# Window graph block and inverted residual on one core: the self part by chunk, w1 rows computed once, and the last depthwise tap as a GpSimd product added by DMA

## What is computed

```python
y = affine(conv1x1(x, fc1_w, fc1_b), fc1_s, fc1_t)
idx = top 9 neighbours of each node by cosine distance   # the node itself is one of them
feat = concat([x_i, x_j - x_i])                          # 9 neighbours j of each node i
h = max over the 9 of gelu((feat @ ew + eb) * es + et)   # 192 channels
x1 = affine(conv1x1(h, fc2_w, fc2_b), fc2_s, fc2_t) + x
```

```python
h = relu(bn(w1 @ x1))
h = relu(bn(depthwise 3x3 convolution of h))             # 9 taps per channel
out = x1 + bn(w2 @ h)
```

## Time and profile before

| what | value |
|---|---|
| median of 3 runs | 4308.5 us (4302.23 to 4312.94) |
| the profiled execution, own time | 4302.27 us |
| its span | 4300.5 us |
| TensorE clock granted, mean | 0.992 |
| PE busy, matmuls | 4078.2 us, 26688 instructions |
| DVE busy | 4077.2 us, 5296 instructions |
| ACT busy | 3620.3 us, 7141 instructions |
| POOL busy | 538.3 us, 548 instructions |
| HBM read and written | 77.68 MB and 25.69 MB |

### The profile page before, as it was taken

The page is one execution under the profiler, slowest core; times in us unless marked ns, Lnnn a source line. Parts: engine busy times, 40 slices in busy tenths (PEclk is TensorE's granted clock), DMA queues, the critical chain, the costliest instruction groups (busy, mean ns, idle before and its releaser), DMA issues.

```text
span 4300.5 us, 84159 instructions
## 1 busy us (share of the span) xinstructions
PE 4078.2 (95%) x26688; PEld 2423.2 (56%) x26688; DVE 4077.2 (95%) x5296; ACT 3620.3 (84%) x7141; POOL 538.3 (13%) x548
## 2 busy tenths in 40 slices
PE   5999999999999999999999999999999999999994
PEld 2555555555555555555555555555555555555552
DVE  2599999999999999999999999999999999999998
ACT  3888888888888888888888888888889888888873
POOL 0011111011111011111011111111111111110100
PEclk9999999999999999999999999999999999999997
DMA  1111121111111111120111111111111111211111
GB/s 48 23 31 33 25 45 18 33 38 30 35 31 31 27 38 32 26 44 16 36 36 24 43 27 32 29 33 34 29 40 20 37 33 25 45 18 25 31 21 24
DMA packets 52989, 134.11 MB, mean 31 GB/s; under 512 B 7778, under 2 KB 9058, under 8 KB 46372
## 3 DMA queue, kind: packets, MB, share of 16 engines
q0 software_dynamic: 28672, 50.35, 8.2%
q1 hardware_dynamic: 23876, 78.22, 6.8%
HBM read 77.68 MB, written 25.69 MB: 24 GB/s over the span
## 4 chain that ended last, share of the span: by engine, by line
PE 61%; ACT 13%; issue 12%; DVE 12%; DMA 0%; SPq 0%; DVEq 0%; ACTq 0%; POOL 0%; POOLq 0%
PE pg L572 15%; DVE acc L954 9%; PE pmisc L498 8%; PE pmisc L482 8%; PE pg L575 7%; PE pvu L559 7%; ACT MV L746 3%; PE pself L586 3%; ACT acc L779 2%; PE pmisc L450 2%; ACT g L763 2%; PE pmisc L500 2%; PE pvu L545 2%; PE pmisc L443 2%; PE pmisc L465 1%
## 5 line engine op out<-in xcount | busy, mean ns | idle before, releaser
L954 DVE SCALAR_TENSOR_TENSOR acc<-hpad,w,acc 128x1024 f32<-128x1024 f32 (+1 forms) x2560 | 2911.9, 1168 | 89.1 <-ACT acc L779 86.0
L572 PE MATMUL pg<-MV,VU 128*128 128x512 f32 x2048 | 1143.8, 640 | 15.6 <-ACT VU L754 14.8
L763 ACT ACTIVATE g<-pg 128x512 f32<-128x512 f32 x1536 | 916.0, 596 | 144.3 <-PE pg L575 75.7
L941 DVE TENSOR_REDUCE hid<-g 128x192 f32<-128x1728 f32 x512 | 992.9, 1939 | 0.0
L746 ACT ACTIVATE MV<-pvu,cst 64x512 f32<-64x512 f32 x1024 | 695.6, 679 | 12.4 <-PE pvu L545 0.2
L482 PE MATMUL pmisc<-x,w 96*128 96x384 f32 (+1 forms) x1536 | 571.6, 487 | 23.1 <-ACT hpad L693 18.5
L575 PE MATMUL pg<-MV,VU 128*64 128x512 f32 x2048 | 527.5, 592 | 0.0
L498 PE MATMUL pmisc<-acc,w 128*96 128x256 f32 x2048 | 494.8, 385 | 30.2 <-ACT acc L786 30.2
L693 ACT ACTIVATE hpad<-pmisc,sh,sc 128x384 f32<-128x384 f32 (+1 forms) x768 | 480.6, 661 | 20.1 <-DVE acc L954 12.7
L559 PE MATMUL pvu<-wVU,y 97*64 97x192 f32 x4096 | 446.6, 339 | 30.6 <-ACT MV L746 30.1
L498 PEld LDWEIGHTS pmisc<-acc,w 128*96 128x96 f32 x2048 | 331.2, 164 | 212.4 <-issue 108.6
(11 more groups left out here) (95 smaller groups left out, 4231.9 us busy)
## 6 DMA issues: line engine op xcount, KB each, us to landing
xin<-in_x_dram SPq DMA_DIRECT2D x32, 768.0 KB, 5.7
invb<-rows_dram SPq DMA_DIRECT2D x32, 768.0 KB
x<-in_x_dram POOLq DMA_DIRECT2D x128, 192.0 KB, 3.6
res<-x POOLq DMA_DIRECT2D x128, 192.0 KB, 3.5
out_dram<-res SPq DMA_DIRECT2D x128, 192.0 KB, 2.1
g<-in_consts_dram SPq DMA_DIRECT2D x1, 640.0 KB
w<-in_p_dram SPq DMA_DIRECT2D x1, 618.5 KB
rows_dram<-norm_rows SPq DMA_DIRECT2D x32, 16.0 KB, 1.4
```

The costliest lines, as they stand in the source:

```text
L572: last = nc.tensor.matmul(ps[:, :], VU[:, r, part, 0:ONE128], cols[part], start=True, stop=True)
L763: nc.scalar.activation(g[:, p % 2, part, :, 0:KN], pg[(3 * p + part) % 2][:, :].rearrange("p (n k) -> p n k", k=KN), ACT.Gelu).then_inc(ge ...
L941: nc.vector.tensor_reduce(hid[:, c % 2, j, :, :], g[:, r], op=ALU.max, axis=AX.X).then_inc(hid_ready, 1)
L954: nc.vector.scalar_tensor_tensor(out=dst, in0=src, scalar=wk, in1=dst, op0=ALU.mult, op1=ALU.add).then_inc(tap_done, 1)
```

## The change

Three things are changed, and the tables of the order with them.

**Self part by chunk.** The third matrix of `wVU` holds the weight of the self term. `self_full` and `self_half` become misc jobs, one of each per chunk instead of per pair: 512 columns from `y` at once, and twice 256 columns. ACT's Gelu writes them to `gself`. `maxima` reads eight columns (1536 elements), and a new DVE instruction per chunk, `join_self`, takes the maximum of `hid` and `gself` (768 elements, both in SBUF). `fc2` waits for that.

**w1 rows once.** A full group gets two jobs of 8 rows (512 columns) for rows 1 to 16 below the strip's top, and the two rows above come from the strip before: POOL copies them within `hpad` (`keep`), and for the half group two DMAs of the SP queue do it. In an image's first strip a job with m = 2 computes row 0 (64 columns).

**Tap 8 of the four full groups.** POOL multiplies `hpad` by the weight (`tap_product`, 1024 elements) into one of two buffers `tapped`, and an accumulating DMA adds that to `acc` (`add_product`) after DVE's tap 7. `relu2` waits for the DMA. The half group keeps its tap 8 on DVE.

```diff
-W1_AT = {-1: [(0, 0), (0, 1)], 0: [(0, 2), (1, 0)], 1: [(1, 1), (1, 2)], 2: [(2, 0), (2, 1), (2, 2)],
-         3: [(3, 0), (3, 1), (3, 2)], 4: [(4, 0), (4, 1)]}
-TAP0_AT = {4: [2], 5: [4]}
-TAP0_LATE = {0: [0], 1: [1], 4: [3]}
-RELU2_AT = {6: [0], 7: [1], 10: [2], 11: [3, 4]}
+W1_AT = {-1: [(0, 0), (0, 1), (0, 2)], 0: [(1, 0)], 1: [(1, 1), (1, 2)], 2: [(2, 0), (2, 1), (2, 2)],
+         3: [(3, 0), (3, 1), (3, 2)], 4: [(4, 0), (4, 2)]}
+KEEP_AT = {-2: (0, 1), 2: (2, 3)}
+UPPER_AT, LOWER_AT = {2: FULL}, {5: FULL}
+TAP0_AT = {}
+TAP0_LATE = {0: [0], 1: [1], 3: [2], 4: [3], 5: [4]}
+RELU2_AT = {6: [0], 7: [1], 10: [2, 4], 11: [3]}
-TAP_COUNTS = [5, 4, 5, 5, 5, 5, 6, 5]
-ORDER = ('ssq', 'fc1', 'inv', 'fc2', 'w1', 'w2')
+TAP_COUNTS = [5, 4, 4, 5, 5, 5, 4, 4]
+PRODUCT_AT = {1: 0, 2: 1, 6: 2, 7: 3}
+SUM_AT = {5: (0,), 6: (1,), 9: (2, 3)}
+SELF_AT = {2: 'self_half', 3: 'self_full', 4: 'self_half', 5: 'self_full'}
+ORDER = ('ssq', 'fc1', 'inv', 'self_full', 'self_half', 'fc2', 'w1', 'w2')
-FIRST = [(g, k) for k in range(1, TAPS) for g in (0, 1)]
-SECOND = [(g, k) for k in range(1, TAPS) for g in (2, 3, 4)]
+FIRST = [(g, k) for k in range(1, TAPS - 1) for g in (0, 1)]
+SECOND = [(2, 1), (3, 1), (2, 2), (3, 2), (4, 1), (2, 3), (3, 3), (4, 2), (2, 4), (4, 3), (3, 4), (2, 5), (4, 4), (3, 5),
+          (2, 6), (4, 5), (3, 6), (2, 7), (4, 6), (3, 7), (4, 7), (4, 8)]
@@ POOL
+            def keep(t, s, gr):
+                if due(count := last_tap(s - 1, gr)):
+                    pool.wait_ge(tap_done, count)
...
+                    nc.gpsimd.tensor_copy(hpad[:, gr, 0:2, :], hpad[:, gr, STRIP:STRIP + 2, :]).then_inc(kept, 1)
+            def tap_product(b, p, o, t, s, gr):
+                fb, fp = when(b, p, o - w1_slot(*w1_last(t, gr)))
+                pool.wait_ge(misc_evac, job_at(fb, fp, "w1", w1_last(t, gr)))
...
+                if due(count := 16 * (s if gr < 2 else s + 1)):
+                    pool.wait_ge(tap_sum[(gr + 2) % FULL], count)
...
+                nc.gpsimd.tensor_scalar(tapped[:, gr % 2, :].rearrange("p (row col) -> p row col", col=W),
+                                        hpad[:, gr, 2:2 + STRIP, 2:2 + W], wd[:, gr, TAPS - 1:TAPS], None,
+                                        ALU.mult).then_inc(product_done, 1)
+            def add_product(t, s, gr):
+                pool.wait_ge(product_done, FULL * s + gr + 1)
+                pool.wait_ge(tap_done, last_tap(s, gr))
+                nc.gpsimd.dma_start(acc[:, t % 2, gr, :], tapped[:, gr % 2, :],
+                                    accum_op=ALU.add).then_inc(tap_sum[gr], 16)
@@ PE
+                elif kind == "self_full":
+                    last = nc.tensor.matmul(ps[:, :], wVU[:, 2, 0:ONE128], y[:, c, :], start=True, stop=True)
+                elif kind == "self_half":
+                    for w in range(2):
+                        last = nc.tensor.matmul(ps[64 * w:64 * w + 64, 0:PPC * NODES].rearrange("p (q n) -> p q n", q=PPC),
+                                                wVU[:, 2, ONE128:O], yc[:, :, w, :], start=True, stop=True)
@@ ACT
+                    nc.scalar.activation(dst, src, ACT.Gelu).then_inc(misc_evac, 1)
...
+                        elif m == 1:
+                            act.wait_ge(kept, FULL * s + gr + 1)
...
             def relu2(s, par, gr):
+                if gr < FULL:
+                    act.wait_ge(tap_sum[gr], 16 * (s + 1))
@@ DVE
+            def join_self(b, p, bc, c):
+                dve.wait_ge(misc_evac, job_at(fb, fp, "self_full", c))
+                nc.vector.tensor_tensor(hid[:, c % 2], hid[:, c % 2], gself[:, c % 2], ALU.max).then_inc(chunk_ready, 1)
```

More of the change, by code:

```diff
@@ L88, in misc_jobs @@
         jobs.append(("inv", bi, c0 + INV_AT[q]))
+    if p % SLOTS in SELF_AT and valid(b, B):
+        jobs.append((SELF_AT[p % SLOTS], b, p // PPC))
     if p % 4 == 1:
@@ L95, in misc_jobs @@
     for _, t, s, parts in due_in(W1_AT, b, p):
-        jobs += [("w1", t, s, part) for part in parts]
+        jobs += [("w1", t, s, part) for part in parts if part[1] < 2 or t == 0]
     jobs.sort(key=lambda job: ORDER.index(job[0]))
@@ L569, in gather @@
                 r = p % 2
-                cols = [MV[:, r, w, 0:KN * NODES] for w in range(2)]
+                cols = [MV[:, r, w, :] for w in range(2)]
                 if part < 2:
@@ new lines, in shared_evac @@
+                        act.wait_ge(kept_half, 32 * s + 16)
+                        nc.scalar.activation(hpad[64:128, gr, 9, 1:W + 1], zrow[64:128, :], ACT.Copy)
+                        for h, n in ((0, 8), (64, 7)):
+                            last = nc.scalar.activation(
+                                hpad[h:h + 64, gr, 2:2 + n, 1:W + 1],
+                                ps[h:h + 64, 0:n * W].rearrange("p (row col) -> p row col", col=W),
+                                ACT.Relu, bias=sh[h:h + 64, :], scale=sc[h:h + 64, :])
@@ L717, in shared_evac @@
+                        last.then_inc(misc_evac, 1)
                 else:
```

212 lines of the change are left out of this document (116 added, 96 removed).

## The result

The changed kernel takes 4315.9 us (median of 13 runs, 4310.1 to 4318.7), the kernel before 4308.5 us (13 runs): a ratio of 1.0021, 95% interval 1.0014 to 1.0029. That is no gain at all, where 4105 us was forecast and 4040 to 4235 us given as the range.

What follows compares the result with a forecast made beforehand. PE and DVE were taken to bound together, each 95% busy. PE 60.4 and DVE 60.6 us with 0.9 idle gave a strip of 61.5, 3.2 less: -198 us, tail -5, so 4105 us; range 4040 to 4235.

Steps and rivals of the forecast that it cites:

- PE, forecast 60.4 us per strip: PE's busy time per strip: self products, w1 and row 0 jobs together -2.75 us, from 63.1 to 60.4.
- DVE without products, forecast 58.6: DVE's busy time per strip: taps -4.8, `maxima` -1.65, join +1.75, from 63.2 to 58.5; row copies +0.1.
- What POOL does to DVE: POOL's products and DVE's taps exclude each other; products cost DVE 0.52 us each, four times, +2.0 us per strip.
- h - 0.19: DVE's loss when a product of length h (0.95 us) meets taps; 0.19 us is absorbed in the next tap's start.
- Idle time, forecast 0.9 instead of 1.5: Time per strip lost to hand-overs between PE and DVE, taken as 0.9 us instead of 1.5, giving a strip of 61.5.
- Fewer extremes: Reason for less idle time: five taps stand where six stood, and the join stands where DVE has room.
- third rival: A new wait once per strip, as `keep`, sum or join before `fc2` comes late; PE stands 1 us; 4165 us, chance 0.11.
- the tail, forecast at -5 us: End of the run: DVE loses eight taps (-9 us) and gets a DMA in its path (+4 us).
- The second (a slower product): Rival: products take h about 1.5 us, half again the copy's rate; DVE 62.5, strip 63.2; 4210 us, chance 0.18.
- The first, free products: Rival: products become ready mostly beside `maxima` and cost DVE nothing; DVE 58.5, PE bounds; 4065 us, chance 0.17.
- the 0.02 for no change: Chance 0.02 given to a time within 0.3% (13 us) of the kernel before.
- A product over 2 us beside `maxima`: Listed as a sign of a wrong forecast, ahead of DVE at 99% with PE under 94% (second or fourth rival).

Runs made afterwards that it cites:

- e1: The changed kernel with one added wait: POOL starts a product only when the same slot's features are done, as DVE enters `maxima`; 4154.5 us.
- e2: The changed kernel with products of 128 instead of 1024 elements (2 of 16 rows), all accumulating DMAs kept; 4159.7 us.
- e7: The changed kernel with the added wait of e1 and `fc2` moved behind the w1 jobs in `ORDER`; 4082.6 us.
- e3: The changed kernel with the four products made by ACT instead of POOL, which still issues the DMAs; 4193.1 us.
- e4: The changed kernel with tap 8 of the four groups back on DVE, without product and DMA; 4290.4 us.
- e8: The kernel before with the self part by chunk alone, w1 in three jobs and tap 8 on DVE; 4279.1 us.
- e9: The changed kernel with only `fc2` moved behind the w1 jobs in `ORDER`, no added wait; 4266.4 us.
- e10: The changed kernel with products put ahead of the DMA issues in POOL's slot (in slot 1 behind `add_product`), no added wait; 4223.0 us.
- e6: The changed kernel with a POOL copy in place of the multiply, so the last tap goes unweighted, no added wait; 4287.5 us.
- e5: The changed kernel with the added wait on `top8_ready`, two taps and the index search ahead of the features; 4235.0 us.
- e12: The changed kernel with product 3 alone put ahead of the DMA issue that adds x1; 4289.2 us.

## Why the prediction was wrong, step by step

**PE, forecast 60.4 us per strip: right.** Where DVE doesn't hold it up it is busy 60.4 (e1), 60.3 (e2) and 60.05 us (e7). The 61.6 of the change are the same work with 140 us of it at half clock: 70 us over 61 strips, 1.15 each.

**DVE without products, forecast 58.6: 0.3 too low.** e2 and e3 show 58.9. Four taps are worth 4.66 us (e4 less e3), not 4.8. `maxima` and join together add 0.26 us (e8) and not 0.10. The join was priced rightly: its record is 958 ns, but from start to start it takes 0.88 us. The rest is that it stands behind a short wait, so that `maxima` ahead of it no longer overlaps with its neighbour's record.

**"What POOL does to DVE", forecast +2.0: this step failed.** (By its own formula it was 4 x 0.52 = 2.1.) Measured is 62.24 - 58.9 = 3.3 us per strip. Two things in it were taken wrongly, and one luckily. The product takes 2.84 us, not 0.95. But its hold of the port is some 0.8 us where it starts from idle, and there the formula's h - 0.19 = 0.76 us meets the measured 0.66 us. It is right because 0.95 us was the time that a POOL instruction keeps a tap off, and wrong as the product's duration. What the formula lacked is the queue. It let a product fall anywhere in DVE's slot, with a chance of 0.61 to meet taps; in fact product 0 starts in `maxima` in 59 of 61 strips (0.04 us) and the other three meet taps nearly always (17 of 183 without excess), as the two queues seem to move in step. And part of these three are caught in the chain of copy, DMA issue and product, where a tap loses up to 2.3 us instead of 0.66. The means are 1.03 + 1.05 + 1.34 = 3.4, what DVE's busy time shows.

**Idle time, forecast 0.9 instead of 1.5: this step failed too.** It became 64.66 - 62.24 = 2.4 us. "Fewer extremes" was the argument, and the change made new ones: a tap of 2.85 us directly ahead of the features, PE's wait behind it, and the half clock. The join's own wait for `maxima`, 21.8 us of 3000 or 0.47 per strip, stood in no term. Of the 1.5 us too few, 0.8 are the wait for the join before `fc2` (e9), the third rival's mechanism. Another part comes with the blocked taps: in e10 the strip's idle time on DVE is down to 1.8 us and the stretches at half clock from 26 to 1.

The sum closes: 61.5 + 0.3 + 1.3 + 1.5 = 64.6, measured 64.66. Over 62 strips that is 192 us. The other 18 us are the tail, forecast at -5 us. From the 508th pair's scores to the end it takes 194.0 us instead of 181.2. It doesn't take a product for that (192.7 in e4, but 186.1 in e8 and 184.9 in e3); which wait it is was not tried.

**The rivals.** None was it alone. The second (a slower product) had DVE's loss nearly right, 4.0 against 3.3, for a wrong reason: e6 shows that the product's length doesn't set the loss. (Its 0.98 us per product belongs to h = 1.54; for 1.5 the formula gives 0.95.) The third was real. The first, free products, is what e7 reaches by aligning them: its strip was worked out as 61.0, and e7 has 60.9. The error behind the 0.02 for no change lies here. Each rival was priced alone against an unchanged rest, while two of them and a larger idle term came true together; that sum is the kernel's old time.

By the estimate from the page "GPSIMD Engine Reference" of the Trainium skill, section "Elementwise — side-by-side cycle accounting", a product takes 1.54 us. The measured 2.84 us are nearly twice that. By the Trainium skill's page "SBUF — State Buffer", section "SBUF: two separate sides", whichever of the two starts first gets the port for its whole instruction. By that rule each product beside taps would have cost 2.84 - 0.19 = 2.65 us. The trace of e5 disagrees: a whole tap fits into the last 1.9 us of a product, and the mean excess there is 0.66 us.

**What was marked as telling right from wrong.** "A product over 2 us beside `maxima`" came true, and was to mean that DVE is at 99% and PE under 94%. DVE was at 93%, so that sign was read from a case in which one engine bounds; two engines that wait for each other have both at 93%.

**How far the causes are shown.** That products beside taps cost the kernel most of its gain is shown by e1 (moved), e2 (made short) and e3 (moved to another engine). That most of e1's remaining idle time was the join is shown by e7. Which strips lose 0.66 and which 2.12 us is read from traces; no run took the copy L475 away from ahead of the product. How much the half clock takes by itself is not: e6 has 27 stretches and e12 12, and they take the same time although DVE is held off longer in e6 as well (247 against 198 us with the features); in e10 it is held off longer than in e5 (159 against 126 us), with 1 stretch against 17, and e10 is 12 us faster. e4 and e8 have 11 and 12 stretches without any product. No two runs differ in the half clock alone. It always came together with the waits that bring it.

## What to carry to other kernels

Work moved to GpSimd beside a full VectorE is priced by where it falls and what stands ahead of it in its own queue more than by its length: over the same 1024 elements, a copy of 1.5 us held VectorE off as long as a multiply of 3.4. Look above all for a GpSimd copy with more work directly behind it. If VectorE has an instruction that is not held off (here a reduction with one SBUF input), make GpSimd wait for the instruction ahead of it; here an added wait brought 161 us. When two engines bound together, price the new waits as a sum and not one at a time, and look for the one instruction that others wait for (here the features). That a delay ahead of it costs more than elsewhere is not shown: e12 shortened that delay by 0.9 us in 30 strips and gained 27 us, no more than its size.
